# ScalarE's order at the group boundaries of two attention layers

## The reference

```
def gat_layer(x, src, dst, W, a_s, a_d, b, concat):
    h = (x @ W).reshape(N, H, C)
    alpha_s = jnp.einsum('nhc,hc->nh', h, a_s)
    alpha_d = jnp.einsum('nhc,hc->nh', h, a_d)
    logits = jax.nn.leaky_relu(alpha_s[src] + alpha_d[dst], 0.2)
    m = jax.ops.segment_max(logits, dst, num_segments=N)
    e = jnp.exp(logits - m[dst])
    s = jax.ops.segment_sum(e, dst, num_segments=N)
    a = e / s[dst]
    out = jax.ops.segment_sum(h[src] * a[:, :, None], dst, num_segments=N)
    return (out.reshape(N, H * C) if concat else out.mean(axis=1)) + b
...
h = gat_layer(x, src, dst, W1, as1, ad1, b1, concat=True)
out = gat_layer(h, src, dst, W2, as2, ad2, b2, concat=False)
```

## Time and profile before

| what | value |
|---|---|
| median of 3 runs | 3591.15 us (3590.56 to 3596.0) |
| the profiled execution | 3587.35 us, of which the span of its instructions 3585.5 us |
| DVE busy over the span | 2253.2 us (63%) |
| POOL busy | 2333.2 us (65%) |
| PE busy, ACT busy | 1175.5 us (33%), 1172.6 us (33%) |

### The profile page before, as it was taken

How to read it: one execution, slowest core, us unless ns; L and a number is a source line. 1 busy time by engine, 2 the same in 40 slices (tenths; PEclk the granted TensorE clock), 3 DMA queues, 4 the chain that set the end, 5 groups by cost and what they waited for, 6 DMA issues and landing times. The chain is left out here.

```text
span 3585.5 us, 33479 instructions
## 1 busy us (share of the span) xinstructions
PE 1175.5 (33%) x5638; PEld 870.0 (24%) x5638; DVE 2253.2 (63%) x4830; ACT 1172.6 (33%) x3423; POOL 2333.2 (65%) x2220
## 2 busy tenths in 40 slices
PE   0555555472122055633552000000000008882221
PEld 0444444362122044521221000000000006661221
DVE  4877777577577477836995333336884436557553
ACT  0666666421223145513552222221000006551110
POOL 6777777777772577327752777774027767772777
PEclk9877877755555555556876555555555559785555
DMA  2677777642111144424662555552001117771000
GB/s 49 204 220 216 222 220 217 202 131 59 42 45 40 41 123 134 122 67 121 201 187 81 151 154 152 153 148 79 0 19 34 48 49 223 218 224 45 18 18 17
DMA packets 247009, 420.84 MB, mean 117 GB/s; under 512 B 75747, under 2 KB 83251, under 8 KB 245677
## 3 DMA queue, kind: packets, MB, share of 16 engines
q1 hardware_dynamic: 176014, 354.96, 32.3%
q0 software_dynamic: 70912, 65.07, 9.2%
HBM read 185.19 MB, written 236.81 MB: 118 GB/s over the span
## 5 line engine op out<-in xcount | busy, mean ns | idle before, releaser
L230 POOL DMA_INDIRECT edge_rows<-x_rows,norm_s x400 | 431.6, 1079 | 141.1 <-issue 121.3
L804 PE MATMUL banks<-ident,cross_in 125*65 125x125 f32 (+4 forms) x26 | 11.2, 431 | 1145.5 <-DVE cross_in L827 751.6
L246 POOL DMA_INDIRECT out_dram<-n_out,scat_i x200 | 224.1, 1120 | 129.0 <-DVE n_out L2145 67.0
L246 POOL DMA_INDIRECT x_rows<-r_x,src_scat_i x200 | 222.6, 1113 | 125.5 <-DVE r_x L2050 63.4
L804 PEld LDWEIGHTS banks<-ident,cross_in 125*65 125x65 f32 (+4 forms) x26 | 3.9, 150 | 1151.1 <-DVE cross_in L827 753.9
L634 DVE TENSOR_REDUCE n_var<-n_sq 125x8 f32<-125x512 f32 x125 | 85.7, 686 | 306.9 <-ACT n_sq L648 306.8
L230 POOL DMA_INDIRECT edge_rows<-in_x_dram,dst_i x200 | 221.0, 1105 | 60.9 <-issue 60.9
L907 DVE TENSOR_TENSOR_SCAN x_t<-x_t 125x144 f32<-125x144 f32 x500 | 202.1, 446 | 82.5 <-ACT x_t L898 74.7
L230 POOL DMA_INDIRECT tops<-norm_rows,src_i x200 | 208.4, 1042 | 68.9 <-issue 67.4
L246 POOL DMA_INDIRECT norm_rows<-edge_rows,scat_i x200 | 208.7, 1043 | 67.9 <-issue 64.5
L230 POOL DMA_INDIRECT edge_rows<-x_rows,key_i x200 | 198.8, 994 | 77.4 <-issue 60.6
(11 more groups left out here) (451 smaller groups left out, 4685.5 us busy)
## 6 DMA issues: line engine op xcount, KB each, us to landing
h_rows<-r_h SPq DMA_DIRECT2D x125, 462.0 KB
x_rows<-r_x SPq DMA_DIRECT2D x125, 241.5 KB
x_rows<-r_x SPq DMA_DIRECT2D x125, 224.0 KB
r_x<-x_rows SPq DMA_DIRECT2D x125, 224.0 KB
x_rows<-n_out SPq DMA_DIRECT2D x125, 224.0 KB
n_in<-in_x_dram SPq DMA_DIRECT2D x100, 224.0 KB
x_mixed_edge_rows<-e_dup SPq DMA_DIRECT2D x50, 448.0 KB
r_x<-x_rows SPq DMA_DIRECT2D x50, 241.5 KB
```

What stands on the lines that cost most here:

```text
L230: g.indirect_dma_start(out=to[:, j, :], out_offset=None, in_=table, in_offset=bass.IndirectOffsetOnAxis(ap=idx[:, j:j + 1], axis=0)).then_ ...
L246: g.indirect_dma_start(out=table, out_offset=bass.IndirectOffsetOnAxis(ap=idx[:, j:j + 1], axis=0), in_=frm[:, j, :] if len(frm.shape) == ...
L804: pe.transpose(crossings["bank"][0:cols, 0:rows], frm, ident[0:rows, 0:rows]).then_inc(s_tout, 1)
```

## The change

On ScalarE alone, at the start of every group but the first, the order changes. Ahead of it stood, behind the two exponentials of the group: in s1 the bank copy of the last chunk of the group ahead and the evictions of its last two chunks; in s2 the square and root of its last chunk. Now in s1 the first factors of the group come first, then that bank copy, the group's first own rows, and one eviction; the other eviction comes one chunk later, behind the bank copy of the group's first chunk. In s2 the first factors and own rows come first, then the square and root. No instruction is added or taken out.

```diff
                     merged_act(act, s1, n)
+                    act.wait_ge(s1.exps, 2 * n + 2)
+                    factors_act(act, s1, start, start)
                     if n:
                         turned_chunk(start - 1)
-                        row_chunk(start - 2)
-                        row_chunk(start - 1)
-                    act.wait_ge(s1.exps, 2 * n + 2)
-                    factors_act(act, s1, start, start)
                     act.wait_ge(s1.args, 3 * n + 3)
                     own_chunk(start)
+                    if n:
+                        row_chunk(start - 2)
                     for i in range(start, end - 1):
                         factors_act(act, s1, i + 1, start)
                         own_chunk(i + 1)
                         turned_chunk(i)
-                        if i > start:
+                        if i:
                             row_chunk(i - 1)
...
                     merged_act(act, s2, n)
-                    if n:
-                        norm_chunk(start - 1)
                     act.wait_ge(s2.exps, 2 * n + 2)
                     factors_act(act, s2, start, start)
                     act.wait_ge(s2.args, 3 * n + 3)
                     own_chunk(start)
+                    if n:
+                        norm_chunk(start - 1)
```

## The result

Nine runs of each kernel give a median of 3569.91 us for the changed one (3564.92 to 3588.45) and 3596.0 us for the one before (3590.56 to 3613.75). The ratio is 0.9928 with a 95% interval of 0.9904 to 0.9951: 26 us faster, between 18 and 35. The forecast was 30 us off and a time of 3561 us, within 3554 to 3568. The gain lies in the direction and nearly in the size that was forecast; the time lies 2 us above the range.

The account below looks back on a forecast made before the run. VectorE was taken to wait 40.7 us in the first layer for factor copies on ScalarE, itself idle before an unrelated semaphore. Gains of 29.2 and 0.8 us took 30.0 from 3591.15, giving 3561 us, range 3554 to 3568.

Parts of the forecast that it names:

- the term of 1.0 us gained at the start at chunk 14: First layer: of the 7.15 us wait there at most 1.7 arrive, cut to 1.0 by slower gather issues.
- the base of three runs: Median of 3591.15 us for the kernel before, from which 30.0 us were taken to give 3561.
- the rival that the change does nothing: Scan L907 was not really waiting for copies L898; time within 0.2% of before; chance 3%.
- The chain inside a group: First layer, times from group start T: nothing VectorE needs comes late; 3.9 us spare for own rows, 4.4 for third chunk's factors.
- another wait takes the place: Own rows or third chunk's factors come late at some group starts, 12 to 15 us lost, about 3575; chance 5%.
- slower: Deferred eviction chain of 11.8 us doubles if TensorE needs twice as long, delaying third chunk's factors: 3598 us; chance 3%.
- The rate of 1/6 us per us of VectorE's work: First layer: each us of VectorE's work delays gather issues by about 1/6 us, 0.7 us at chunk 14.
- 29.2: First layer's gain in us, summed over group starts at chunks 9, 14, 19, 23 and the end: 0 + 1.0 + 8.79 + 9.31 + 10.05.
- The tail behind it: First layer, last chunk's end to the barrier: stays as long as before, so the chunk's gain reaches the program.
- more than forecast: Over 34 us gained, with TensorE at the higher clock level in the tail; chance 3%.
- The gather rival: First layer: all gather issues take 1.5 us, chunk 14's group starts 4.4 us later than before; total gain 24.6, 3566.6; chance 10%.
- The gain of 0.8 us: Second layer: VectorE's waits for factors at the last two group boundaries go, 0.8 us, bounds 0 and 0.8.

Follow-up runs that it names:

- factors_only: Kernel before, with only the first factors of a group moved ahead in the first layer; own rows stay late: 3580.7 us, ratio 0.9972.
- evict_both: Changed kernel with both evictions right behind a group's first own rows in the first layer; 8.5 us of waits expected: 3571.25 us, ratio 0.9955.
- s1_only: Kernel before with only the first layer's part of the change: 3562.8 us, ratio 0.9940.
- no_mixed_store: Changed kernel without the first layer's store of mixed rows and its waits; the gather reads another table: 3565.93 us, ratio 0.9935.
- no_add: Changed kernel without the adding of own rows in the first layer but for one column, result wrong: 3537.11 us, ratio 0.9856.
- s2_only: Kernel before with only the second layer's part of the change: 3589.43 us, ratio 1.0005.
- again: The changed kernel run once more, unaltered, for a second profile: 3564.47 us, ratio 0.9937.
- even groups: Changed kernel with groups cut at chunks 0, 5, 9, 13, 17, 21 instead of 0, 4, 9, 14, 19, 23: 3556.93 us, ratio 0.9912; 3557.61 us on another chip.

## Why the prediction was right and where it was not

The mechanism held: the waits for factors went, none took their place, and the gather took back part of the gain. What failed is the term of 1.0 us gained at the start at chunk 14, which was a loss of 1.3 to 3.3 us, and the base of three runs from which the time was counted. Both are taken up below.

**The cause and what goes.** Right. L907's wait for L898 went from 40.7 us to none in the first layer and the block became shorter, so the rival that the change does nothing is out. The wait did hide another one: factors_only shows 25.7 us for own rows, and the change moved those too.

**The chain inside a group.** Right to 1.4 us. Behind the start at chunk 14 (T = 1403.50): own rows end at T + 9.9 (10.0 forecast), the first chunk at T + 15.15 (15.2), the deferred eviction at T + 11.1 (11.4), the factors of the third chunk at T + 21.0 (22.4), ahead of the scan at T + 26.8 (26.8). No new wait on ScalarE appeared. evict_both takes away one margin of this chain and shows 8.4 us of waits where it says 8.5. That was the point on which "another wait takes the place" and "slower" turned, and both fell with it.

**What arrives of the 40.7 us.** The mechanism was right, the term of the start at chunk 14 was mis-sized. It said: landed 2.49 us behind the last issue, which slips by 0.7 us, so T = 213.3 us behind the first issue and 1.0 us gained. Measured: last issue at 212.3 instead of 210.8, landing 4.1 us behind it, T = 216.3; the second profile has 211.2, 4.4 and 215.7, and s1_only, with the same order in this layer, 213.2, 4.5 and 217.7. So 1.3 to 3.3 us were lost against before (214.4) instead of 1.0 gained. Two parts of it:
- *The landing* (1.6 to 2.0 us). I took 2.49 us from the only start that waited for its gather visibly in the profile of before, and at that one SP's queue had long been idle. Where VectorE has just ended a chunk, two stores and a load stand ahead of the last gathers. no_mixed_store brings 2.49 back at both starts.
- *The issues* (0.4 to 2.3 us). The rate of 1/6 us per us of VectorE's work took all of its instructions alike. no_add shows that the adds cost about 0.8 us per us of theirs (20 of 26). That this made the issues late here is not tested. s2_only, with the old order in the first layer, already has the last issue at 211.7 and starts this group at 217.1 without a wait, so two executions of the old order differ by as much as this term.

The starts at chunks 19 and 23 and the end followed as forecast: T to T 51.8 and 41.7 us, then 22.9, no waits. In sum the first layer gave 26.0 us in the first pair of profiles where 29.2 stood, and 26.9 us in the mean of three profiles with the new order against two with the old, counted to the end of the last L1669. The tail behind it is 41.2 us before and after, as forecast. The rival *more than forecast* named TensorE at the higher clock level in the tail: s2_only shows such a tail, worth 4.7 us, in a kernel with the old order.

Of the signs named in advance, VectorE waits for the gather 8.1 us at chunk 9 and 7.1 us at chunk 14, where about 5 and 5 to 6 were expected, and not at 19 or 23; the last L1669 ends 26 us earlier and not 29.

The gather rival was thus partly true, by a mechanism that its text named only in half: the starts came no later than it allowed (its 4.4 us were 1.3 to 3.3), and it was longer landings as much as longer issues.

**The second layer.** The 0.8 us of waits for factors are gone, the wait for the root is 0.9 us as before: those steps hold. The gain of 0.8 us did not arrive. Among the profiles with the groups of before, the block takes 364.4 to 365.4 us in the old order (three) and 365.2 to 368.6 with the edit (seven). In the profile of again 3.0 of the 4.1 us more are there at the start at chunk 14, where VectorE waits 2.9 us for the landing instead of 0.3. All seven profiles with the edit start this group at 204.1 to 206.2 us behind the block's first gather issue, the three without at 203.0 to 203.9. With even groups VectorE waits for no landing at the start of a later group in this layer, and there is no difference. I took the landings there as given, and why they come later with the edit is open. In the times the edit can't be seen (1.0005, 0.9988 to 1.0022), which does not exclude 2 us.

**The time itself.** 3561 was 3591.15, the median of three runs, less 30. The median of nine runs of the kernel before is 3596.0. Of the 8.9 us between 3561 and 3569.9, 4.9 are the base and 4 the gain. The range took in the scatter of the result's own runs too narrowly at the upper end: unchanged blocks scatter by up to 18 us between executions. The same kernel gave 3564.47 us in again, inside the range, so on which side of the bound 2 us away a sample of runs falls is luck.

## What to carry to other kernels

An engine that is waited for and is itself idle in front of a semaphore is the cheapest thing to mend: move what doesn't depend on the awaited event ahead of that wait, then look which of its next results would be late (here own rows, then the second eviction), and move those too. Before counting such a gain, take at each place the next arrival that can bind, and take its delay from a place with the same traffic ahead of it, not from a quiet one. When the new bound is the arrival of a group, the size of the groups is the next knob.

## What the runs showed of the hardware that I had not expected

- A landing that took 2.49 us behind the issue of the last gather took 4.1 to 4.5 us at six starts where SP had begun to issue 1285 KB of stores and loads 2.9 us ahead of it, and 2.49 us again in the one profile with 500 KB of these left out and the rest issued earlier.
- Forty VectorE adds with two inputs in SBUF, 26 us of busy time, lengthened 200 gather issues on GpSimd by 20 us in total. 65 us of scans and 82 us of multiplies between the same issues were left in place in a kernel with a surplus of only 12.7 us.
- The same tail of 41.2 us took 36.5 us in a profile where TensorE's granted clock was 0.87 instead of 0.50 in 10 us of it.
- Blocks with identical instructions took 1630 to 1648 us in different executions, more than half of the gain under study.
